# In the last shared-expert group GpSimd splits two weight chunks ahead of the first token gather, and the turns' place in SyncE's load loop moves by two indices

## The chip, the cores and the metric

The kernel runs on one core of a Trainium2 chip. The metric is device time of one execution in microseconds (us). Before the change three runs gave 1834.8, 1836.18 and 1836.39 us, median 1836.18.

The core has five engines, each with an instruction stream of its own, held together by semaphores alone: TensorE (PE; its weight loads are shown as PEld), VectorE (DVE), ScalarE (ACT), GpSimd (POOL) and SyncE (SP), which here only issues DMAs. POOL issues DMAs too: those with indices, and those that add to what is in memory. SPq and POOLq stand for the issuing side of these two engines. An engine works strictly in order: an instruction that waits holds up all that stand behind it.

## The reference, cut to what matters

A decoder layer over x (8 batches, 512 tokens each, width 512), float32:

```
x = x + attn(layernorm(x), queries, combiners)
x = x + cross_attention(layernorm(x), ctx, Wq, bq, Wk, bk, Wv, bv)
x = x + ffn(layernorm(x))
ffn(y):  t = y as 4096 tokens
         probs = softmax(t @ router_w + router_b);  the 2 best of 16 experts per token, weights normed to sum 1
         each expert takes its first 640 tokens: out_e = (silu(h @ w_gate) * (h @ w_up)) @ w_down
         result = y + shared expert(y) + the weighted outputs of the two experts of each token
```

The hidden width is 704. Reaching the precision of float32 takes three matmul passes: each operand is split into a high and a low part, and high*high, high*low and low*high are summed.

## The kernel before, in words

Phase 1 is the attention part. Phase 2 is the feed-forward part. It is a list of 24 groups (`groups`, line 1080). Groups 0 to 7 run the shared expert (job 0) over the 8 batches of 512 tokens. Groups 8 to 23 run the 16 experts (jobs 1 to 16) over 640 gathered tokens each. Every group has six gate/up steps c = 0..5 (matmuls at L72) and then a down projection (L1522) for each tile of 128 tokens. In a step, ACT takes silu of the gate out of PSUM (L1378), DVE multiplies it with up (L1440), ACT writes the high half of the product (`h_hi`, line 1356), and DVE the low half (`h_lo`, line 1417, profile line L1424). The `h_hi` and `h_lo` of step c stand behind silu and product of step c+1. PE's down projection waits for the low half of each step (line 1516).

A job's weights are 17 chunks of 256 KB (`WC`; 11 for gate/up, 6 for down). A chunk n is loaded into one of `RAW` = 6 raw buffers by SP (`load_weights`, line 1234, profile line L1240), its high half is written by ACT (`split`, line 1338, profile line L1336) and its low half by POOL (`split`, line 1276, profile line L1278) into one of `RING` = 22 ring slots. SP's load of chunk n waits until POOL has split chunk n-6 (line 1236). `split_after` (line 1166) gives what is split after which step of which group. In group 7, the last of job 0, chunks 22 and 23 are split after step 0, 24 and 25 after step 1, 26 and 27 after step 2, 28 and 29 after step 3, 30 and 31 after step 4, 32 after step 5, and 33 to 38 after the down projection. ACT does a step's splits one step later: those of step 3 stand behind the `h_hi` of step 3 and in front of silu of step 5 (lines 1386 to 1388). Chunks 22 to 27 have been loaded since SP's turn at group 5 (lines 1258 to 1260). Group 8 needs chunks 17 to 27 for gate/up and 28 to 33 for down.

The tokens of the first expert come so: DVE writes the slot of each token, POOL scatters (token, weight) pairs into a table `slots` (L469), SP reads the table back as `slot_list` (line 1263), POOL gathers the rows of five tiles of 128 tokens by five indirect DMAs (`gather`, line 1284, L1291), SP turns them by five transposing DMAs (`turn_tokens`, line 1216, L1222), and ACT and DVE rebuild float32 halves of them between the down tiles (L1408, L1414, and ACT under L1336). The gather of group 8 (`gather(B)`) stands ahead of all of group 7's splits on POOL. The later gathers stand at the start of the group before.

SP's last loop (lines 1265 to 1270) runs over n = 22, 23, ...; at index i of a job it calls `turn_tokens`, and from n = RING + RAW on it calls `load_weights(n)`.

Of the kernel before, what the change touches and what calls it, by code (L numbers as in the profile page):

```python
# [40 lines left out]
B, S, D = 8, 512, 512  # L41
NT = S // P
# [3 lines left out]
E, K, F = 16, 2, 704  # L46
# [987 lines left out]
def phase2(nc, ctx, a, Y, shared, at, attn):  # L1034
# [7 lines left out]
    TURN_AT = RAW + 4  # L1042

    def sem(name):
        return ctx.enter_context(nc.semaphore(name))
# [29 lines left out]
    s_list = sem("t_list")  # L1075
# [90 lines left out]
    def split_after(g, step):  # L1166


        job, _, _, last = groups[g]
        if g == 0 and step == 3:  # L1170
            return list(range(FIRST, WC))
        if (g, step) in RING_REST:
            return [WC + RING_REST.index((g, step))]
        if not last:
            return []
        done = range(GU, WC) if step == "down" else range(2 * step, min(2 * step + 2, GU))
        return [job * WC + i + RING for i in done if job * WC + i + RING < n_chunks]
# [10 lines left out]
    def adds_of(g, t):  # L1188

        return sum(tiles > t for tiles in tiles_of[:g])  # L1190
# [22 lines left out]
    def sync(sp):  # L1213
        step = attn["sync"](sp)

        def turn_tokens(g):
            sp.wait_ge(s_xg, 16 * gathered[g + 1])
            if gathered[g]:
                sp.wait_ge(s_xtop, gathered[g])
                sp.wait_ge(s_xlow, gathered[g])  # L1220
            for t in range(ET):
                sp.dma_start_transpose(xp[t][:], xn[:, t, :]).then_inc(s_xp, 16)  # L1222

        def load_tokens(g):
            if g == 1:
                filled(sp, "SC", B - 1, NT - 1)
                filled(sp, "V", B - 1, NT - 1)
            else:
                sp.wait_ge(attn["s_ttop"], NT * g)
                sp.wait_ge(attn["s_tlow"], NT * g)  # L1230
                sp.wait_ge(s_gu, unit_no[(g - 2, FC - 1, 0)] + 1)
            step("TURN", g)

        def load_weights(n):
            if n >= RAW:
                sp.wait_ge(s_wl, n - RAW + 1)
            elif n == 0:
                filled(sp, "M", B - 1)
            job, i = divmod(n, WC)
            sp.dma_start(wraw[n % RAW][:], a["wts"][job, :, i * D:(i + 1) * D]).then_inc(s_raw[n % RAW], 16)  # L1240

        for name, b in order:
            if name == "RAW":
                for n in range(RAW):
                    load_weights(n)
            elif name == "WEIGHTS":
                for n in range(*b):
                    load_weights(n + RAW)
            elif (name, b) == ("TURN", 1):
                load_tokens(1)  # L1250
            else:
                step(name, b)
        for stored in attn["s_yout"]:
            sp.wait_ge(stored, 16 * NT * B // 2)
        sp.wait_ge(attn["s_out"], 16 * B)
        for g in range(2, B):
            load_tokens(g)
            if g == 5:
                for n in range(RING, RING + RAW):
                    load_weights(n)  # L1260

        sp.wait_ge(attn["s_scat"], 16 * K * NT * B)
        sp.dma_start(slot_list[:].rearrange("p (e t) k -> p e (t k)", e=E),
                     slots.rearrange("(e p t) k -> p e (t k)", e=E, t=ET)).then_inc(s_list, 16)
        for n in range(RING, n_chunks):
            job, i = divmod(n - RING, WC)
            if i == (0 if job == 0 else TURN_AT) and job < E:
                turn_tokens(B + job)
            if n >= RING + RAW:
                load_weights(n)  # L1270
        sp.wait_ge(attn["s_out"], 16 * B)

    def gpsimd(pool):
        step = attn["gpsimd"](pool)

        def split(n):
            pool.wait_ge(s_wh, n + 1)
            pool.tensor_tensor(wl[n % RING][:], wraw[n % RAW][:], wh[n % RING][:].bitcast(F32),  # L1278
                               ALU.subtract).then_inc(s_wl, 1)

        def rows_at(e, t):
            return bass.IndirectOffsetOnAxis(ap=slot_list[:, e * ET + t, 0:1].bitcast(U32), axis=0)

        def gather(g):

            if g == B:
                pool.wait_ge(s_gu, unit_no[(B - 2, FC - 1, 0)] + 1)
            else:
                pool.wait_ge(s_xp, 16 * gathered[g])
            for t in range(ET):  # L1290
                pool.indirect_dma_start(xn[:, t, :], None, Y[:, :], rows_at(groups[g][1], t),  # L1291
                                        bounds_check=N + PAD - 1).then_inc(s_xg, 16)

        for name, b in order:
            if name == "WEIGHTS":
                for n in range(*b):
                    split(n)
            elif name not in ("RAW",):
                step(name, b)
        for g, (job, part, tiles, last) in enumerate(groups):  # L1300
            if g >= B and g + 1 < NG:
                gather(g + 1)
            if g == B - 1:
                for stored in attn["s_yout"]:
                    pool.wait_ge(stored, 16 * NT * B // 2)
                pool.wait_ge(s_list, 16)
                gather(B)
            for c in range(FC):
                for n in split_after(g, c):
                    split(n)  # L1310
                if (g, c) in scatter_after:
                    step("SCATTER", scatter_after[g, c])
            for t in range(tiles):
                pool.wait_ge(s_ost, tiles_before[g] + t + 1)
                if job == 0:

                    pool.wait_ge(attn["s_out"], 16 * (part + 1))
                    pool.dma_start(out[part * S + t * P:part * S + (t + 1) * P, :], ost[:, t, :],
                                   accum_op=ALU.add).then_inc(s_add[t], 16)
                    continue  # L1320
                if t == 0:

                    for i in range(ET):
                        pool.wait_ge(s_add[i], 16 * adds_of(g, i))
                pool.indirect_dma_start(out[:, :], rows_at(part, t), ost[:, t, :], None,  # L1325
                                        bounds_check=N + PAD - 1, compute_op=ALU.add).then_inc(s_add[t], 16)
            for n in split_after(g, "down"):
                split(n)
        for i in range(ET):
            pool.wait_ge(s_add[i], 16 * adds_of(NG, i))  # L1330
# [194 lines left out]

    block = ctx.enter_context(nc.Block())
    block.sync(sync)
    block.gpsimd(gpsimd)
    block.scalar(scalar)
    block.vector(vector)  # L1530
# [46 lines left out]
```

## Time and profile before

| | |
|---|---|
| three runs, us | 1834.8, 1836.18, 1836.39 (median 1836.18) |
| profiled execution, us | 1836.62 |
| its span from first to last instruction, us | 1834.9 |
| PE busy | 1819.7 us, 99% |
| PEld busy | 1613.0 us, 88% |
| DVE busy | 843.8 us, 46% |
| ACT busy | 754.5 us, 41% |
| POOL busy | 887.1 us, 48% |
| mean granted clock of TensorE | 0.998 |

Group 7 runs on PE from 848.8 to 896.1 us. The timeline view lists merged runs of like instructions: start, length, engine, line, operation, output<-input, count, and in brackets the idle time before it with what ended it. The chain of waits is followed back from the last instruction: start, length, what.

### The profile page before, as it was taken

To read this page: it belongs to the slowest core of one execution; us is meant where nothing else is said; L and a number is where in the kernel's file an instruction comes from. 1 tells how busy PE (TensorE), PEld (TensorE's weight loads), DVE (VectorE), ACT (ScalarE), POOL (GpSimd) and SP (SyncE) were. 2 spreads that over 40 slices of the span, in tenths; PEclk is the share of its full clock that TensorE was granted. 3 is DMA by queue.
4 is the path that set the end of the run, shared out by engine and by line. 5 is a ranking of instruction groups with operands and counts; after the bars stand their busy time and mean duration, and the time that the engine had idled before them with its cause. 6 is when DMAs were issued, how large, how long until landed. Compare 5 with 4: busy or idle time off the path is not lost.

```text
span 1834.9 us, 27134 instructions
## 1 busy us (share of the span) xinstructions
PE 1819.7 (99%) x10104; PEld 1613.0 (88%) x10104; DVE 843.8 (46%) x2028; ACT 754.5 (41%) x1490; POOL 887.1 (48%) x760
## 2 busy tenths in 40 slices
PE   9999999999999999999999999999999999999997
PEld 6888888888887887888899999999999999999996
DVE  6667656765765344343344233442344323443242
ACT  4544434444554333332444434443344434444331
POOL 2443444335553232224655666555665656556631
PEclk9999999999999999999999999999999999999999
DMA  8431342233452233223766666676666676666722
GB/s 311 167 105 65 126 144 98 81 110 110 115 138 40 37 41 81 47 46 60 184 125 153 155 148 140 127 164 152 141 143 131 163 153 134 144 139 164 144 41 29
DMA packets 216274, 219.90 MB, mean 120 GB/s; under 512 B 133680, under 2 KB 133680, under 8 KB 214864
## 3 DMA queue, kind: packets, MB, share of 16 engines
q1 hardware_dynamic: 190848, 165.07, 32.8%
q0 software_dynamic: 25296, 53.11, 16.9%
q8 instruction: 80, 1.31, 0.3%
q14 instruction: 50, 0.41, 0.1%
HBM read 138.80 MB, written 49.97 MB: 103 GB/s over the span
## 4 chain that ended last, share of the span: by engine, by line
PE 93%; issue 4%; DMA 1%; SPq 1%; DVE 0%; POOL 0%; ACT 0%; POOLq 0%; DVEq 0%; ACTq 0%
PE ps L72 64%; PE ps L1522 22%; PE ps L866 4%; PE ps L872 1%; PE ps L1007 1%; PE ps L891 1%; DMA slot_list<-slots 0%; SPq L1222 0%; SPq L353 0%; DMA buffer<-in_wts 0%; DMA buffer<-tokens_normed,slot_list 0%; PE ps L967 0%; POOL buffer L1291 0%; DMA buffer<-in_WkT 0%; PE ps L943 0%
## 5 line engine op out<-in xcount | busy, mean ns | idle before, releaser
L72 PE MATMUL ps<-buffer,buffer 128*128 128x320 f32 (+1 forms) x6900 | 1240.5, 341 | 1.2 <-DVE buffer L719 0.8
L72 PEld LDWEIGHTS ps<-buffer,buffer 128*128 128x128 f32 x6900 | 1120.6, 188 | 106.8 <-issue 1.5
L1278 POOL TENSOR_TENSOR buffer<-buffer,buffer 128x512 fp32r<-128x512 f32 x289 | 379.4, 1478 | 250.1 <-ACT buffer L1336 249.8
L1522 PE MATMUL ps<-buffer,buffer 128*128 128x512 f32 x1904 | 437.8, 390 | 1.4 <-DVE buffer L1424 1.4
L1522 PEld LDWEIGHTS ps<-buffer,buffer 128*128 128x128 f32 x1904 | 355.7, 188 | 76.1 <-POOL buffer L1278 2.2
L1336 ACT ACTIVATE buffer<-buffer 128x512 fp32r<-128x512 f32 (+1 forms) x491 | 294.3, 652 | 166.2 <-PE ps L1522 93.7
L1378 ACT ACTIVATE buffer<-ps 128x320 f32<-128x320 f32 (+1 forms) x240 | 112.7, 469 | 598.6 <-PE ps L72 571.0
L1440 DVE TENSOR_TENSOR ps<-ps,buffer 128x320 f32<-128x320 f32 (+2 forms) x198 | 100.2, 506 | 490.5 <-ACT buffer L1378 462.7
L1325 POOL DMA_INDIRECT out_tokens<-buffer,slot_list x80 | 125.8, 1573 | 185.6 <-DVE buffer L1470 137.3
L469 POOL DMA_INDIRECT slots<-pairs,slot_u x64 | 63.6, 994 | 182.0 <-DVE slot_u L853 164.9
L477 ACT ACTIVATE buffer<-ps 128x512 fp32r<-128x512 f32 (+1 forms) x148 | 81.9, 603 | 107.6 <-PE ps L72 59.8
L482 ACT ACTIVATE buffer<-buffer,shift,rstd 128x512 f32<-128x512 f32 x96 | 70.6, 808 | 102.8 <-DVE shift L647 102.8
L1470 DVE TENSOR_SCALAR buffer<-ps,slot_list 128x512 f32<-128x512 f32 x80 | 59.7, 746 | 112.2 <-PE ps L1522 112.2
L1424 DVE TENSOR_TENSOR buffer<-ps,buffer 128x320 fp32r<-128x320 f32 (+2 forms) x198 | 96.8, 489 | 10.2 <-ACT buffer L1336 9.2
L442 POOL TENSOR_TENSOR buffer<-buffer,buffer 128x512 f32<-128x512 f32 x32 | 42.1, 1351 | 116.2 <-DVE shift L647 105.4
L1291 POOL DMA_INDIRECT buffer<-tokens_normed,slot_list x80 | 83.6, 1046 | 29.7 <-issue 29.7
L1336 ACT ACTIVATE buffer<-ps 128x320 fp32r<-128x320 f32 (+2 forms) x198 | 86.5, 437 | 0.3 <-DVE ps L1440 0.3
L1440 DVE TENSOR_TENSOR buffer<-ps,buffer 128x512 f32<-128x512 f32 (+1 forms) x42 | 29.0, 690 | 97.7 <-ACT buffer L1378 93.5
L1408 DVE COPY buffer<-buffer 128x512 uint16<-128x512 uint16 x80 | 73.1, 936 | 0.5
L431 POOL TENSOR_TENSOR buffer<-buffer,buffer 128x512 fp32r<-128x512 f32 x28 | 35.2, 1298 | 71.8 <-ACT buffer L477 71.8
L629 DVE BATCH_NORM_STATS2 stats<-buffer 128x6 f32<-128x512 f32 x96 | 61.3, 685 | 7.9 <-DMA buffer<-in_x 7.3
L477 ACT ACTIVATE buffer<-buffer 128x512 fp32r<-128x512 f32 (+1 forms) x104 | 59.8, 679 | 3.9 <-DMA buffer<-in_ctxT 2.2
(126 smaller groups left out, 1058.1 us busy)
## 6 DMA issues: line engine op xcount, KB each, us to landing
buffer<-in_wts SPq DMA_DIRECT2D x289, 256.0 KB
buffer<-in_xT SPq DMA_DIRECT2D x8, 1024.0 KB, 5.5
buffer<-in_ctxT SPq DMA_DIRECT2D x8, 1024.0 KB, 7.8
out_tokens<-buffer SPq DMA_DIRECT2D x8, 1024.0 KB, 4.4
tokens_normed<-buffer SPq DMA_DIRECT2D x32, 256.0 KB, 2.8
out_tokens<-buffer POOLq DMA_DIRECT2D x32, 256.0 KB, 5.6
buffer<-in_x SPq DMA_DIRECT2D x7, 1024.0 KB, 5.4
buffer<-combiners_top SPq DMA_DIRECT2D x6, 1024.0 KB, 7.6
```

The lines of the kernel that those rows point to most:

```text
L72: last = pe.matmul(out, left, right, start=(c == 0 and i == 0), stop=(c == len(parts) - 1 and i == 2))
L477: return act.activation(dst, src, ACT.Copy)
L866: last = pe.matmul(out, left, right, start=(i == 0), stop=(i == len(pairs) - 1))
L1278: pool.tensor_tensor(wl[n % RING][:], wraw[n % RAW][:], wh[n % RING][:].bitcast(F32), ALU.subtract).then_inc(s_wl, 1)
L1291: pool.indirect_dma_start(xn[:, t, :], None, Y[:, :], rows_at(groups[g][1], t), bounds_check=N + PAD - 1).then_inc(s_xg, 16)
L1325: pool.indirect_dma_start(out[:, :], rows_at(part, t), ost[:, t, :], None, bounds_check=N + PAD - 1, compute_op=ALU.add).then_inc(s_add[t] ...
L1336: return act.activation(dst, src, ACT.Copy)
L1378: act.activation(silu[u % TMP][0:rows_of(c), 0:n], bank[0:rows_of(c), 0:n], ACT.Silu)\
L1408: dve.tensor_copy(halves_of(t)[:, :, :, 0], xp[t][:, NC:2 * NC, :]).then_inc(s_xlow, 1)
L1424: dve.tensor_tensor(lo[:, first:first + n], product_of(u)[0:rows, 0:n], hh[0:rows, c, first:first + n].bitcast(F32), ALU.subtract).then_in ...
L1440: dve.tensor_tensor(product_of(u)[0:rows_of(c), 0:n], up_bank[u % 2][rows, 0:n], silu[u % TMP][0:rows_of(c), 0:n], ALU.mult).then_inc(s_ht, 1)
L1522: ins = pe.matmul(down_bank[n % 2][:], left, right, start=(c == 0 and i == 0), stop=(c == FC - 1 and i == len(passes) - 1))
```

## The change

On POOL the block that waits for the stored tokens and for `slot_list` and then issues `gather(B)` moves from the head of group 7 to behind the splits that belong to step 0 of group 7, which are those of chunks 22 and 23. On SP the index at which `turn_tokens(B)` is called in the last loop changes from 0 to 2.

```
@@ sync
         for n in range(RING, n_chunks):
             job, i = divmod(n - RING, WC)
-            if i == (0 if job == 0 else TURN_AT) and job < E:
+            if i == (2 if job == 0 else TURN_AT) and job < E:
                 turn_tokens(B + job)
             if n >= RING + RAW:
                 load_weights(n)
@@ gpsimd
             if g >= B and g + 1 < NG:
                 gather(g + 1)
-            if g == B - 1:
-                for stored in attn["s_yout"]:
-                    pool.wait_ge(stored, 16 * NT * B // 2)
-                pool.wait_ge(s_list, 16)
-                gather(B)
             for c in range(FC):
                 for n in split_after(g, c):
                     split(n)
+                if (g, c) == (B - 1, 0):
+                    for stored in attn["s_yout"]:
+                        pool.wait_ge(stored, 16 * NT * B // 2)
+                    pool.wait_ge(s_list, 16)
+                    gather(B)
                 if (g, c) in scatter_after:
                     step("SCATTER", scatter_after[g, c])
```

## Rows read from the trace of the kernel before

**Rows 1.** The page, busy time by engine and the chain's shares.
```profile
PE 1819.7 (99%) x10104; PEld 1613.0 (88%) x10104; DVE 843.8 (46%) x2028; ACT 754.5 (41%) x1490; POOL 887.1 (48%) x760
PE 93%; issue 4%; DMA 1%; SPq 1%; DVE 0%; POOL 0%; ACT 0%; POOLq 0%; DVEq 0%; ACTq 0%
```
**Rows 2.** Timeline of PE, end of group 7; in brackets idle time before.
```profile
878.71 2.88 PE L1522 MATMUL ps<-buffer,buffer 128*128 128x512 f32 x12
882.70 0.93 PE L1522 MATMUL ps<-buffer,buffer 128*128 128x512 f32 x3 [1.10 <-DVE buffer L1424]
883.97 12.28 PE L1522 MATMUL ps<-buffer,buffer 128*128 128x512 f32 x53 [0.34 <-DVE buffer L1424]
```
**Rows 3.** Chain of waits in order of time (start, us, what), 845 to 882.
```profile
849.55 9.13 DMA slot_list<-slots
...
865.16 3.80 DMA buffer<-tokens_normed,slot_list
...
877.35 4.62 DMA buffer<-in_wts
```
**Rows 4.** Timeline of SP's queue, 845 to 880.
```profile
868.97 6.76 SPq L1222 DMA_TRANSPOSE buffer<-buffer  x5
875.78 3.17 SPq L1240 DMA_DIRECT2D buffer<-in_wts  x6
```
**Rows 5.** Timeline of ACT in group 7.
```profile
860.90 1.16 ACT L1336 ACTIVATE buffer<-buffer 128x512 fp32r<-128x512 f32 x2
...
871.79 1.15 ACT L1336 ACTIVATE buffer<-buffer 128x512 fp32r<-128x512 f32 x2
...
879.13 0.64 ACT L1336 ACTIVATE buffer<-buffer 128x512 fp32r<-128x512 f32 x1 [1.78 <-DMA buffer<-in_wts]
...
880.45 0.58 ACT L1378 ACTIVATE buffer<-ps 64x512 f32<-64x512 f32 x1
```
**Rows 6.** Timeline of POOL, 848 to 882.
```profile
859.70 1.15 POOL L1291 DMA_INDIRECT buffer<-tokens_normed,slot_list  x1 [7.65 <-issue]
...
865.16 1.01 POOL L1291 DMA_INDIRECT buffer<-tokens_normed,slot_list  x1 [0.30 <-issue]
866.20 5.04 POOL L1278 TENSOR_TENSOR buffer<-buffer,buffer 128x512 fp32r<-128x512 f32 x4
872.50 2.54 POOL L1278 TENSOR_TENSOR buffer<-buffer,buffer 128x512 fp32r<-128x512 f32 x2 [1.26 <-ACT buffer L1336]
```
**Rows 7.** Timeline of POOL at the next gather, that of group 9.
```profile
897.84 7.85 POOL L1278 TENSOR_TENSOR buffer<-buffer,buffer 128x512 fp32r<-128x512 f32 x6
905.87 1.12 POOL L1291 DMA_INDIRECT buffer<-tokens_normed,slot_list  x1 [0.17 <-issue]
```
**Rows 8.** Line L1222 (the turns), issue to landing; timelines of DVE and PE.
```profile
DMA to landing us min/median/max: 3.1/3.3/3.4
...
883.86 2.77 DVE L1408 COPY buffer<-buffer 128x512 uint16<-128x512 uint16 x2
893.04 0.69 DVE L1414 TENSOR_TENSOR buffer<-buffer,buffer 128x512 fp32r<-128x512 f32 x1
...
896.09 38.88 PE L72 MATMUL ps<-buffer,buffer 128*128 128x320 f32 x264
```
**Rows 9.** Timeline of PE at its end; windows there (stretch, us, busy, PEclk, DMA).
```profile
1819.66 4.69 PE L1522 MATMUL ps<-buffer,buffer 128*128 128x512 f32 x20
...
1826.00:1827.00 1.00, 0.00 (x0) 0.00 (x0) 0.00 (x0) 0.00 (x0) 1.00 (x1) 1.00 0.19 31
1827.00:1828.00 1.00, 0.00 (x0) 0.00 (x0) 0.00 (x0) 0.00 (x0) 0.48 (x1) 0.61 0.00 0
1828.00:1834.00 6.00, 0.00 (x0) 0.00 (x0) 0.00 (x0) 0.00 (x0) 0.00 (x0) 0.50 0.34 44
```
**Rows 10.** Timeline of PE at the kernel's start.
```profile
1.08 3.17 PE L878 MATMUL ps<-ones 128*128 128x128 bf16 x28 [1.08 <-POOL ones L377]
4.49 11.49 PE L891 MATMUL ps<-buffer,buffer 128*128 128x512 f32 x26 [0.24 <-DMA buffer<-in_WkT]
```

More of the change, by code:

```diff
@@ L1266, in sync @@
             job, i = divmod(n - RING, WC)
-            if i == (0 if job == 0 else TURN_AT) and job < E:
+            if i == (2 if job == 0 else TURN_AT) and job < E:
                 turn_tokens(B + job)
@@ L1302, in gpsimd @@
                 gather(g + 1)
[L1303 to L1307, printed above, removed]
             for c in range(FC):
@@ L1310, in gpsimd @@
                     split(n)
+                if (g, c) == (B - 1, 0):
+                    for stored in attn["s_yout"]:
+                        pool.wait_ge(stored, 16 * NT * B // 2)
+                    pool.wait_ge(s_list, 16)
+                    gather(B)
                 if (g, c) in scatter_after:
```

## The prediction

> **What bounds the kernel now.** I read the page first: PE is busy 99% of the span, and the chain that ended last is 93% PE [rows 1]. So every us by which PE idles longer comes on top, and nothing that POOL, ACT or SP save elsewhere counts unless PE idles there. Then I asked the timeline of PE for the stretch that the change touches. Group 7's gate/up ends where the first 12 down matmuls begin at 878.71. These end near 881.6, PE idles 1.10 us, does 3 matmuls, idles 0.34 us, and then runs through [rows 2]. Both gaps end with DVE's low half of the product. These 1.44 us are PE's only idle time in the group.
>
> The chain of waits says what is behind the gap, and here it leaves PE for 35 us: the read of the slot list (9.13 us from 849.55, landed at 858.68), the gathers, the last of which lands 3.80 us after it started at 865.16, SP's turns, SP's weight loads, one of which lands at 881.97, and behind it ACT and DVE, at whose work PE's gap ends [rows 2, 3]. SP's queue shows the join: five turns from 868.97, the weight loads right behind at 875.78 [rows 4]. The first of them is chunk 28. ACT's timeline shows its use: ACT idles 1.78 us for a landing in_wts chunk and starts its split at 879.13; silu of step 5 comes behind it at 880.45 [rows 5], and the high and low halves of step 4, which PE waits for, come behind that silu. So PE does not need chunk 28 until the down projection of group 8, but ACT, working in order, passes on its lateness at once. The end of this chain has no slack: it is already late by 1.44 us of PE time.
>
> **SP's edit.** The loop starts at n = 22, and load_weights is called from n = 28 on. The iterations 22 and 23 (indices 0 and 1) therefore issue nothing, and neither do 24 to 27. Turns at index 2 stand in the same place of SP's queue as turns at index 0: behind the read of the list, ahead of the load of chunk 28. Cost and gain are 0 from both sides, for the instruction streams are equal. No load goes ahead of the turns.
>
> **POOL's edit, before.** The list is there at 858.68 [rows 3]. The first gather starts at 859.70, the fifth at 865.16 for 1.01 us, so the gathers end at 866.17. Splits 22 to 25 follow in one run of four [rows 6]. The turns start at 868.97, which is 2.80 us after the last gather's end [rows 4, 6].
>
> **POOL's edit, after.** The gather now stands behind splits 22 and 23, which wait for ACT's halves of these chunks. ACT writes them from 860.90, and that is set by PE's pace (behind silu of step 1), not by POOL [rows 5]. Where ACT starts a pair at 871.79, POOL starts its own at 872.50, 0.71 us later [rows 5, 6]. So POOL's split 22 starts at 860.90 + 0.71 = 861.61. Two splits take 2.54 us [rows 6], which gives 864.15. From a split to a following gather whose waits are met it takes 0.18 us (897.84 + 7.85 = 905.69 to 905.87) [rows 7]. The first gather starts at 864.33 and not at 859.70: a shift of 4.63 us. The upper bound is the form seen before, 1.02 us from release to gather, which gives 5.5. The lower bound comes if POOL's splits started with ACT's: 3.9. I take 4.6, for the two rows used are the same instructions with the same neighbours.
>
> **What hangs on the gather.** The five gathers, their landing, the five turns and the loads behind are the same work in the same order, so all move by 4.6: turns from 873.6, load of chunk 28 at 875.78 + 4.63 = 880.4, ACT's split 28 at 883.8 (before 879.13), silu of step 5 at 885.1, and PE's gap ends at 887.3 and not at 882.70. PE still reaches the gap at 881.6, since its first 12 down matmuls need only steps 0 to 3, which are done. The gap is 1.10 + 4.63 = 5.7 us, and the 0.34 behind it stays. Nothing gives it back: before, PE has no more idle time from here on in which it could be saved [rows 2].
>
> What is hidden. Splits 24 to 27 on POOL move behind the gathers: gathers from 864.33 for the same 6.47 us end at 870.8, splits 24 and 25 at 873.3, 26 and 27 at 875.9. Loads up to chunk 33 wait for split 27, and SP comes to them after 880.4, so 4.5 us of cover remain. The turned tokens land at most 3.4 us after issue; before, the last was issued some 5.4 us after 868.97, landing at 877.8; after, at 882.4. DVE's use at 883.86 moves to 888.5. The last low half of them is done at 893.73, PE wants it at 896.09 [rows 8]; both move together and keep 2.4 us. If that cover were gone, PE would wait the difference at the head of group 8, but both hang on the same late `h_lo`.
>
> **The clock.** A gap of 5.7 us on PE is five times the one that is there now [rows 2]. What a long one does can be seen at the end alone: PE's last matmul ends at 1824.35, the granted clock is 1.00 until 1827, has a mean of 0.61 in the next us, which puts the fall near 1827.2, and is 0.50 (1.2 GHz) from then on [rows 9]. PE had been idle for 2.9 us there, and here it would be for 5.7. The price of coming back is seen at the start: 28 matmuls of 128 columns take 3.17 us, 113 ns each, while 53 of 512 columns take 12.28 us, 58 ns per 128 columns [rows 10, 2]. By these durations the stretch ran at half pace (1.2 GHz). Of a stretch of 3.17 us at half pace, half is lost: 1.6 us. Bounds: 0 (the clock holds) and twice that, 3.2 us. I take 1.6, the one stretch that the trace has.
>
> The Trainium skill (TensorE: Matmul & The Clock Gate, "What's actually happening") says of this: "the default state is throttled, and activity releases the throttle". The trace agrees at both ends. Its table of what to do asks for matmuls without long gaps in mid-kernel; no stretch of this trace shows a fall and a recovery in mid-kernel, so by that rule the sum has the clock term, and without it the sum is 4.6.
>
> **Sum.** 4.6 + 1.6 = 6.2 us. On the profiled execution's own time 1836.62 (span 1834.9 and 1.7 around it) that is 1842.8. The median of the runs is 0.44 lower: 1836.18 + 6.2 = 1842.4, or +0.34%. The forecast is slower.
>
> **Rivals.**
>
> A. The late turns without the clock. The gap is there, but the clock holds at 2.4 GHz. For it: the granted clock stays at 1.00 for 2.9 us of idling at the end [rows 9], and where the fall comes may differ between executions. Against it: 5.7 is twice 2.9. Time: 1836.18 + 4.6 = 1840.8.
>
> B. The loads do go in front of the turns, by two. If chunks 28 and 29 were raw before ACT comes to them, ACT would next wait for chunk 30, issued first behind the turns at 880.4 and landing as chunk 28 did 3.35 us after issue [rows 4, 5], at 883.8, with chunk 31 some 0.7 us later; split 31 and the high half of step 5 would end near 885.7, the low half at 886.4. PE would idle 4.1 us before the step-5 matmuls where it now idles 1.44: +2.7, 1838.9. Against it is the plain reading of the loop: n >= 28.
>
> C. Not slower: the wait for the list covers the two splits. POOL idles 7.65 us ahead of the first gather [rows 6]. If the list lands later than POOL's split 23 ends (864.15), the splits fill idle time and the gather starts when it did. It decides from a list that lands 5.5 us later than in the profile. Then the time is 1836.2; and if, besides, an earlier split 24 or an earlier raw buffer took away ACT's wait, at most the whole 1.44 us of PE's gaps could go: 1834.7. Against it: the list landed at 858.68, and the runs' spread of 1.6 us leaves no room for a list 5.5 us later, as that would have lengthened the kernel before by the same chain.
>
> D. The clock costs twice as much: half pace for twice the start's stretch, 1836.18 + 4.6 + 3.2 = 1844.0. For it: the waits around the gap leave PE with 3 matmuls and a further short gap before steady work.
>
> **How the numbers follow.** The forecast 0.49, A 0.26, D 0.08, B 0.06, C 0.11. The forecast's own spread is 1841.3 to 1843.5. The range from 1838.2 to 1844.5 holds the forecast, A, D and B, 0.89 by their chances, and some 0.8 with the uncertainty of their sizes. A measurement of this kernel can tell about 0.2% from no change, that is 3.7 us, so slower means above 1839.85. The forecast, D and most of A lie there: 0.49 + 0.08 + 0.20 = 0.77. Same: the rest of A, B and most of C: 0.06 + 0.06 + 0.08 = 0.20. Faster: 0.03.
>
> **What would show it.** In the changed profile: POOL's timeline has two L1278 from about 861.6, then the first L1291 near 864.3; SP's turns start near 873.6 and the loads follow at once near 880.4, with none between 849.6 and 873; ACT waits some 6.4 us for in_wts and starts at 883.8; PE's gap ahead of the second run of L1522 is 5.7 us; a window over 884 to 892 shows a granted clock under 1 and matmuls near 460 ns. Wrong: a weight load ahead of the turns (B), a list landing past 864 (C), or a gap with clock 1.00 (A). What would upset all is a first gather under 860, or a gap that stays near 1.1 us in spite of late turns.

## The result and the profile after

The changed kernel takes 1843.03 us in the median of 7 runs (1840.93 to 1845.03), against 1835.21 (1834.39 to 1836.39) before. The ratio is 1.0042, 95% interval [1.0032, 1.0052]: slower, by 7.8 us in the medians. The prediction was 1842.4, +6.2, range 1838.2 to 1844.5. The profiled execution took 1843.07 us, span 1841.4.

Timeline of GpSimd in the changed kernel, then of SyncE's queue and of ACT.

```profile
861.59 2.53 POOL L1278 TENSOR_TENSOR buffer<-buffer,buffer 128x512 fp32r<-128x512 f32 x2 [9.56 <-ACT buffer L1336]
864.29 1.14 POOL L1291 DMA_INDIRECT buffer<-tokens_normed,slot_list  x1 [0.17 <-issue]
...
869.77 1.02 POOL L1291 DMA_INDIRECT buffer<-tokens_normed,slot_list  x1 [0.30 <-issue]
870.82 5.04 POOL L1278 TENSOR_TENSOR buffer<-buffer,buffer 128x512 fp32r<-128x512 f32 x4
```

```profile
849.52 0.38 SPq L1263 DMA_DIRECT2D slot_list<-slots  x1
873.63 6.76 SPq L1222 DMA_TRANSPOSE buffer<-buffer  x5
880.45 9.52 SPq L1240 DMA_DIRECT2D buffer<-in_wts  x10
```

```profile
860.88 1.15 ACT L1336 ACTIVATE buffer<-buffer 128x512 fp32r<-128x512 f32 x2
...
883.93 0.63 ACT L1336 ACTIVATE buffer<-buffer 128x512 fp32r<-128x512 f32 x1 [6.62 <-DMA buffer<-in_wts]
884.80 0.63 ACT L1336 ACTIVATE buffer<-buffer 128x512 fp32r<-128x512 f32 x1 [0.24 <-DMA buffer<-in_wts]
885.34 0.57 ACT L1378 ACTIVATE buffer<-ps 64x512 f32<-64x512 f32 x1
```

Against [rows 6], the first gather moved from 859.70 to 864.29. It is preceded by two splits of 1.27 us, and before them GpSimd idles 9.56 us for ACT, whose splits came when they did before (860.88 against 860.90 [rows 5]). Against [rows 4], turns and loads moved from 868.97 and 875.78 to 873.63 and 880.45. No load stands between the slot list and the turns: SyncE's half of the change moved nothing. ACT's wait for chunk 28 grew from 1.78 to 6.62 us. A second wait of 0.24 us, for chunk 29, is new, and silu of step 5 moved by 4.89.

Timeline of PE in the changed kernel, and its granted clock (columns of the windows, here and below: stretch, us, busy and count of PE, PEld, DVE, ACT, POOL, then granted clock, DMA share, GB/s).

```profile
878.69 2.88 PE L1522 MATMUL ps<-buffer,buffer 128*128 128x512 f32 x12
887.58 15.20 PE L1522 MATMUL ps<-buffer,buffer 128*128 128x512 f32 x56 [6.01 <-DVE buffer L1424]
902.62 2.65 PE L72 MATMUL ps<-buffer,buffer 128*128 128x320 f32 x17
```

```profile
884.00:886.00 2.00, 0.00 (x0) 0.00 (x0) 0.00 (x0) 1.76 (x4) 1.36 (x2) 0.87 0.95 347
886.00:888.00 2.00, 0.42 (x1) 0.45 (x2) 1.45 (x3) 2.00 (x5) 2.00 (x2) 0.50 0.87 288
888.00:890.00 2.00, 2.00 (x6) 1.44 (x6) 1.97 (x3) 1.73 (x3) 2.00 (x3) 0.50 0.63 166
890.00:892.00 2.00, 2.00 (x7) 1.52 (x6) 2.00 (x3) 1.85 (x4) 1.05 (x1) 0.50 0.70 231
892.00:894.00 2.00, 2.00 (x9) 1.63 (x8) 1.47 (x3) 1.77 (x4) 1.01 (x1) 0.92 0.48 145
894.00:896.00 2.00, 2.00 (x10) 1.68 (x9) 0.89 (x2) 0.30 (x1) 0.00 (x0) 1.00 0.86 108
```

The gap in the second line answers to the 1.10 us of [rows 2]: it is 6.01 us. The gap of 0.34 in front of step 5's matmuls is gone. Step 5's low half starts 1.20 us after step 4's (DVE at 886.74 and 887.94), and PE, at half clock, takes some 1.4 us over step 4's three matmuls (8 of them take 3.75 us), so it no longer waits. The granted clock falls to 0.50 (1.2 GHz) while PE idles and is back at 1.00 soon after 892. In the stretches of 2 us PE gets 6 and 7 matmuls done and not the 10 of the last line.

One measure serves all runs below: the **down stretch** of group 7, from its first down matmul to the first matmul of group 8. Before: 878.71 to 896.09 = 17.38 us [rows 2, 8]. After: 878.69 to 902.62 = 23.93 us, that is +6.55, of which the gaps account for 6.01 - 1.44 = 4.57 and the slower matmuls for the other 2.0. Counted by place, the first gap adds 4.91, and all behind it (step 4's three matmuls, step 5's gap, the rest up to group 8) 1.65. The spans differ by 6.5, so nothing else of note moved.

### The profile page after: what moved, and what is told of

Read it like the earlier page. It is cut to its first block, busy times and chain, and to the rows that moved or that the text cites. A ratio compares the mean times of both kernels' runs of the same rounds, so it can differ in the third digit from the quotient of the medians.

```text
span 1841.4 us, 27134 instructions
## 1 busy us (share of the span) xinstructions
PE 1822.0 (99%) x10104; PEld 1614.9 (88%) x10104; DVE 843.3 (46%) x2028; ACT 752.9 (41%) x1490; POOL 887.6 (48%) x760
## 4 chain that ended last, share of the span: by engine, by line
PE 96%; DMA 1%; DVE 1%; SPq 1%; issue 1%; POOL 0%; ACT 0%; POOLq 0%; ACTq 0%; DVEq 0%
PE ps L72 66%; PE ps L1522 24%; PE ps L866 4%; PE ps L872 1%; PE ps L1007 1%; DMA buffer<-means 0%; SPq L1222 0%; DMA buffer<-in_x 0%; DMA means<-mean 0%; DMA buffer<-tokens_normed,slot_list 0%; DMA buffer<-in_wts 0%; POOL buffer L1291 0%; DVE buffer L280 0%; PE ps L943 0%; DVE buffer L719 0%
```

## The experiments

All eleven ran with a profile and in five rounds against the kernel before. The medians of before beside them were 1835.2 (sp_only, pool_only, keep_busy, late_splits_after), 1835.21 (the two doses and the two loads_ahead) and 1835.47 (the two loads4 and splits_between). The ratio compares the two kernels over the rounds. In the table, gap is PE's idle time within the down stretch.

| kernel | first gather | gap, us | clock in the stretch | down stretch, us | median, us | ratio [95%] |
|---|---|---|---|---|---|---|
| before (its profile) | 859.70 | 1.10 + 0.34 | 1.00 | 17.38 | 1835.21 | |
| sp_only | 857.38 | 0.15 | 1.00 | 15.85 | 1835.31 | 0.9998 [0.9989, 1.0006] |
| changed kernel | 864.29 | 6.01 | falls | 23.93 | 1843.03 | 1.0042 [1.0032, 1.0052] |
| pool_only | 863.62 | 5.78 + 0.38 | falls | 23.92 | 1842.34 | 1.0034 [1.0021, 1.0047] |
| keep_busy | 863.98 | 0.87 + 0.43 | 1.00 | 22.19 | 1840.76 | 1.0027 [1.0017, 1.0037] |
| dose_one | 862.55 | 4.12 | falls | 21.69 | 1840.82 | 1.0033 [1.0022, 1.0043] |
| dose_four | 869.37 | 11.04 | falls | 29.40 | 1848.10 | 1.0068 [1.0054, 1.0082] |
| loads_ahead_after | 863.49 | 3.62 | falls | 20.95 | 1840.93 | 1.0030 [1.0019, 1.0041] |
| late_splits_after | 864.18 | none; 5.80 in group 8 | 1.00 here, falls in group 8 | 15.44 | 1842.22 | 1.0033 [1.0021, 1.0044] |
| loads4_after | 864.53 | 0.15 + 0.65 | 1.00 | 16.80 | 1836.09 | 1.0001 [0.9992, 1.0010] |
| splits_between | 862.81 | none | 1.00 | 15.42 | 1834.22 | 0.9994 [0.9985, 1.0003] |
| loads_ahead_before | 856.84 | 0.16 | 1.00 | 15.83 | 1834.87 | 0.9997 [0.9988, 1.0006] |
| loads4_before | 858.91 | 0.16 | 1.00 | 15.82 | 1834.67 | 0.9996 [0.9987, 1.0005] |

### The two halves of the change

pool_only is the changed kernel with SyncE's index back at 0; sp_only is the kernel before with index 2.

```
-            if i == (0 if job == 0 else TURN_AT) and job < E:      # sp_only has this edit alone;
+            if i == (2 if job == 0 else TURN_AT) and job < E:      # pool_only has all but this one
```

> Only GpSimd's half of the change; SyncE's turns stay at index 0. Theory (the whole cost comes from the gather behind two splits): the same as the changed kernel, about 1842 to 1844 us, against about 1835.2 before; first gather at 864.3, turns at 873.6, one gap of 6.0 us on PE. Rival (SyncE's edit has a part in it): clearly nearer to 1835.

> Only SyncE's half of the change; the gather stays in front. Theory: the loop issues nothing for its first six indices, so the instruction streams are those of the kernel before: ratio 1.000 within 0.1%, which also gives the noise of a comparison. Rival (two loads do go out in front of the turns, as in rival B): the turns start some 0.9 us later and ACT's wait of 1.78 us for the first chunk goes, up to 1.4 us faster.

pool_only has the full cost, 1.0034, its interval overlapping that of the change, and sp_only has none, 0.9998. The rival for each falls. The second gap of pool_only (0.38 us, at half clock) has its own cause: ACT waits 0.59 us more for a weight chunk in front of the high half of step 5. But sp_only's profile holds what the prediction had not seen. Its instruction streams are those of the kernel before, and its trace differs. Timelines of POOL and PE of sp_only:

```profile
857.38 1.14 POOL L1291 DMA_INDIRECT buffer<-tokens_normed,slot_list  x1 [5.43 <-issue]
```

```profile
878.61 3.56 PE L1522 MATMUL ps<-buffer,buffer 128*128 128x512 f32 x15
882.33 12.29 PE L1522 MATMUL ps<-buffer,buffer 128*128 128x512 f32 x53 [0.15 <-DVE buffer L1424]
894.46 30.81 PE L72 MATMUL ps<-buffer,buffer 128*128 128x320 f32 x209
```

The gather starts 2.3 us earlier than in the profile of before, and PE's gaps are 0.15 us and not 1.44. The cause is the read of the slot list, whose line in the two traces (before, then sp_only) says:

```profile
DMA to landing us min/median/max: 9.1/9.1/9.1
DMA to landing us min/median/max: 6.9/6.9/6.9
```

In sp_only the gather starts 1.02 us behind that landing, as before, and ACT waits for no weight chunk any more. Over the 13 traces of this case the same small transfer took 6.1 to 7.1 us in nine, and 8.5, 8.5, 9.1 and 9.2 in four. The profile of before was one with a late list. The execution that gave sp_only's trace took 1835.20 us, like the median of before; that of before took 1836.62. Against sp_only the change adds 23.93 - 15.85 = 8.1 us to the down stretch, and the medians say 7.8.

### Is the clock a term of the sum?

```
+                    if (g, t, c) == (B - 1, 0, FC - 2):
+                        pe.wait_ge(s_ht, unit_no[(g, FC - 2, 0)] + 1)
+                        for _ in range(KEEP):          # KEEP = 22
+                            pe.matmul(gate_bank[unit_no[(g, FC - 2, 0)] % 2][:], hh[:, 0, cols],
+                                      wh[(base + GU) % RING][:], start=True, stop=True)
                     if t == 0:
                         pe.wait_ge(s_wl, m + 1)
```

> The changed kernel, with 22 more matmuls (of 128x512, results into a bank that is free then, used by nothing) on PE between the down matmuls of steps 3 and 4 of the first tile of group 7, where the gap is. 22 x 0.23 = 5.1 us, less than the gap. Theory (6.0 us of late work plus some 2 us of half clock behind the gap): the granted clock stays at 1.00, PE's idle time falls to about 0.9 + 0.3 us, the 0.34 us gap in front of step 5 comes back, and the time falls by 2 to 3 us to about 1840 (1835.2 + 4.6). Rival (the clock in the record costs nothing, the rest is something else): stays at 1843.

Timeline of PE in keep_busy, and its clock over the same time:

```profile
878.36 2.88 PE L1528 MATMUL ps<-buffer,buffer 128*128 128x512 f32 x12
881.08 5.15 PE L1518 MATMUL ps<-buffer,buffer 128*128 128x512 f32 x22
887.10 0.94 PE L1528 MATMUL ps<-buffer,buffer 128*128 128x512 f32 x3 [0.87 <-DVE buffer L1425]
888.46 12.25 PE L1528 MATMUL ps<-buffer,buffer 128*128 128x512 f32 x53 [0.43 <-DVE buffer L1425]
```

```profile
884.00:888.00 4.00, 3.13 (x13) 1.99 (x11) 1.76 (x3) 3.92 (x8) 3.63 (x3) 1.00 0.85 296
888.00:892.00 4.00, 3.57 (x17) 2.98 (x17) 3.97 (x5) 3.50 (x7) 2.83 (x3) 1.00 0.72 198
```

The work of step 4 resumes as late as in the changed kernel (887.10 against 887.58), the clock holds, the small gap comes back, and the down stretch is 1.7 us shorter than in the changed kernel. The medians differ by 2.3 us from the changed kernel, by 1.6 from pool_only, which ran beside it. From the resumed work to group 8 keep_busy takes 13.45 us and the changed kernel 15.04, which is 1.6. So the clock's term is 1.6 to 2.3 us, shown by an edit that fills the gap and leaves the late chain as it is.

### Does the cost follow the gather's start?

dose_one puts one split ahead of the gather, dose_four four.

```
# dose_one
-                for n in split_after(g, c):
+                for k, n in enumerate(split_after(g, c)):
+                    if (g, c, k) == (B - 1, 0, 1):
+                        (the gather's four lines, as in the change)
                     split(n)
-                if (g, c) == (B - 1, 0):
-                    (the same four lines)
# dose_four
-                if (g, c) == (B - 1, 0):
+                if (g, c) == (B - 1, 1):
```

> As the changed kernel, but only chunk 22 is split ahead of the first gather; 23 comes behind it. Theory: gather at 863.0, all behind it 3.4 us later than before, PE's gap 1.44 + 3.4 = 4.8 us; the clock still falls, for the gap is longer than the 2.9 us of idling after which it fell at the end of the kernel, and costs some 2 us: about 1840.5. Rival (the clock only falls after a gap nearer to 6 us): 1838.6.

> As the changed kernel, but four chunks (22 to 25) are split ahead of the first gather, which then stands behind step 1's splits. Theory: ACT's split 24 starts at 866.3, GpSimd's at 867.0, both done at 869.6, gather at 869.75, that is 10.05 us later than before and 5.45 later than in the changed kernel; PE's gap 11.5 us; the cost of the clock does not grow with the gap, so the time is 1843.0 + 5.45 = 1848.5. Rival (part of the cost is one that does not follow the gather's start): off that line by over 1.5 us.

Timelines of PE, dose_one and then dose_four:

```profile
885.19 14.85 PE L1522 MATMUL ps<-buffer,buffer 128*128 128x512 f32 x56 [4.12 <-DVE buffer L1424]
```

```profile
892.26 15.64 PE L1522 MATMUL ps<-buffer,buffer 128*128 128x512 f32 x56 [11.04 <-DVE buffer L1424]
```

dose_one came out at 1840.82 (expected 1840.5), dose_four at 1848.10 (1848.5). The gap goes 4.12, 6.01, 11.04 with one, two and four splits, while what is lost behind it stays small: 56 matmuls and the way to group 8 take 14.69, 15.04 and 15.48 us (885.19 to 899.88, 887.58 to 902.62, 892.26 to 907.74). So the late start is paid one for one, and the clock about once. Both gaps came out shorter than expected (4.12 for 4.8, 11.04 for 11.5 us). The clock fell in dose_one too, as expected: 0.87 over 884 to 886 and 0.50 over 886 to 888.

### What the change's words say, done

```
             if i == (2 if job == 0 else TURN_AT) and job < E:
+                if job == 0:
+                    for m in range(RING + RAW, RING + RAW + 2):    # loads4_after and loads4_before: + 4
+                        load_weights(m)
                 turn_tokens(B + job)
-            if n >= RING + RAW:
+            if n >= RING + RAW + 2:
                 load_weights(n)
```

> The changed kernel, and SyncE does what the change's words say: it issues the loads of chunks 28 and 29 ahead of the turns. Theory (rival B of the prediction, worked out there): ACT's splits 28 and 29 wait for nothing, the turns start at 873.7, ACT next waits for chunk 30, PE has one gap of some 4 us in front of step 5's matmuls; +2.7 us by the gap, plus up to 2 us of clock if it falls: 1838 to 1840. Rival (any load behind the turns holds ACT as long): 1843.

> The changed kernel (gather behind splits 22 and 23), with the loads of chunks 28 to 31 issued ahead of the turns; the last of them waits for split 25, which ends near 873.3, when the turns would start anyway. Theory (the cost of the late gather is only the lateness of the loads that ACT meets in front of silu of step 5 and the high half of step 5): ACT waits for none of the four; it waits up to 2 us for chunk 32, behind the high half of step 5, where the 2 to 4 us of slack of group 8's tokens cover it; PE's gap is under 0.4 us, clock 1.00, time 1835 to 1836, as before. Rival (the late gather itself, by the tokens, costs time): 1837 or more.

Timeline of PE in loads_ahead_after, and its clock; then PE in loads4_after:

```profile
877.89 3.56 PE L1525 MATMUL ps<-buffer,buffer 128*128 128x512 f32 x15
885.07 13.93 PE L1525 MATMUL ps<-buffer,buffer 128*128 128x512 f32 x53 [3.62 <-DVE buffer L1427]
```

```profile
884.00:886.00 2.00, 0.93 (x4) 0.83 (x5) 1.73 (x3) 1.72 (x4) 2.00 (x3) 1.00 0.98 330
886.00:888.00 2.00, 2.00 (x8) 1.59 (x7) 2.00 (x3) 2.00 (x5) 0.94 (x1) 0.64 0.69 228
888.00:890.00 2.00, 2.00 (x6) 1.52 (x6) 1.36 (x3) 1.85 (x4) 1.01 (x1) 0.51 0.47 137
```

```profile
878.93 3.56 PE L1525 MATMUL ps<-buffer,buffer 128*128 128x512 f32 x15
882.65 4.57 PE L1525 MATMUL ps<-buffer,buffer 128*128 128x512 f32 x19 [0.15 <-DVE buffer L1427]
887.87 8.02 PE L1525 MATMUL ps<-buffer,buffer 128*128 128x512 f32 x34 [0.65 <-DVE buffer L1468]
895.73 9.54 PE L72 MATMUL ps<-buffer,buffer 128*128 128x320 f32 x64
```

Two loads ahead do what rival B said: 15 and not 12 down matmuls run through, then one gap of 3.62 us in front of step 5's (4.1 predicted). The clock falls after this gap too, and the median of 1840.93 lies just above the expected 1838 to 1840. That profiled execution was the fastest of its seven (1839.12), so what its clock cost may not be what it costs in the median.

With four loads ahead no cost can be measured any more, 1836.09 and 1.0001 [0.9992, 1.0010], with the gather as late (864.53) as in the changed kernel. ACT's one wait is 2.30 us for chunk 32, behind the high half of step 5. It shows at PE as 0.65 us between the down tiles: DVE waits 2.48 us for ACT's token half, and its copy L1468, which frees PE's bank, stands behind. The gaps of 0.80 us in all are more than the 0.4 expected, and the down stretch is 0.95 us longer than sp_only's.

### Are late loads harmful by ACT's order alone?

```
         done = range(GU, WC) if step == "down" else range(2 * step, min(2 * step + 2, GU))
+        if g == B - 1 and step in (3, 4, 5):
+            return []
+        if g == B - 1 and step == "down":
+            done = range(6, WC)                                   # chunks 28 to 38
```

> The changed kernel, with the splits of chunks 28 to 32 taken out of group 7's steps 3 to 5 and put at the head of its splits after the down projection, on ACT and GpSimd. The gather, the turns and the loads stay as late as in the changed kernel. Theory (late loads cost only because ACT, in order, waits for chunk 28 in front of silu of step 5): PE's gap goes altogether, clock 1.00, turned tokens land near 882.4, in time; the time is 1835.2 + 0 - 1.4 = about 1834, at most 1835.5. Rival (the late turns themselves hold up the tokens of group 8): the gap moves to the head of group 8 or between the down tiles, 1838 or more.

This expectation failed: 1842.22 is where the rival's number lay (1838 or more). The gap did leave the down stretch, which at 15.44 us is as short as any. It came back in the next group. PE's timeline and the chain of waits of late_splits_after:

```profile
894.02 7.20 PE L72 MATMUL ps<-buffer,buffer 128*128 128x320 f32 x48
907.01 18.28 PE L72 MATMUL ps<-buffer,buffer 128*128 128x320 f32 x110 [5.80 <-DVE ps L1444]
```

```profile
895.21 0.85 POOL out_tokens L1322
896.05 6.30 POOL buffer L1282 x5
902.35 0.02 issue
902.37 3.01 DMA buffer<-in_wts
905.38 0.02 issue
905.40 0.02 ACT buffer L1340
```

I had moved GpSimd's splits behind the output stores as well. The loads of chunk 34 and on wait for GpSimd's split six chunks back, so they were late in their turn, and ACT met them in front of silu of group 8, in order as ever. The chain runs through weights (in_wts) and not through the late tokens, so the rival has the place right and the cause wrong. Both variants of the stall are ACT waiting for a chunk that nobody needs for tens of us. What was wrong is my edit, and the next one mends it: ACT splits one chunk behind each token step, GpSimd splits them in front of the stores.

```
+        if g == B - 1 and step in (3, 4, 5):
+            return [28, 29, 30, 31, 32] if step == 5 else []      # GpSimd: in front of the output stores
...
             for m in split_after(g, FC - 1):                      # ACT
-                split(m)
+                if g != B - 1:
+                    split(m)
...
                     x_hi(gx, t)
+                    if g == B - 1:
+                        split(28 + t)                             # ACT: one behind each token step
```

> The changed kernel, loads as late as there, but chunks 28 to 32 are split by ACT one each behind the five token steps of group 7's tail, and by GpSimd in front of the output stores. It mends what went wrong in the trial that put these splits behind the whole tail, where the six raw buffers came free too late. Theory (order on ACT): no gap in front of step 4's down matmuls; five splits of 0.63 us lengthen the token chain, which may cost PE up to 2 us at the head of group 8 or between down tiles: 1835.2 to 1837.5. Rival (late loads cost wherever the splits stand): 1840 or more.

Timeline of PE in splits_between:

```profile
877.21 15.59 PE L1527 MATMUL ps<-buffer,buffer 128*128 128x512 f32 x68
892.63 12.62 PE L72 MATMUL ps<-buffer,buffer 128*128 128x320 f32 x85
```

All 68 down matmuls run without a gap, group 8 follows at once, and the median is 1834.22, ratio 0.9994 [0.9985, 1.0003], below the band I gave (1835.2 to 1837.5), as the five extra splits lengthened nothing that PE waits for. Loads and turns are as late here as in the changed kernel (turns 5.1 us ahead of PE's first down matmul in both: 872.07 and 877.21, 873.63 and 878.69). So the lateness by itself costs nothing: the 8 us come from the place of the splits. The edit moves those of both engines; that ACT's are the ones that count is read from the changed kernel's trace (its wait of 6.62 us in front of silu), and no run moved ACT's alone.

### Candidates

> The kernel before (gather in front), and SyncE issues the loads of chunks 28 and 29 ahead of the turns. They go out at about 867.5 and 868.7, behind GpSimd's splits 22 and 23, and the turns at about 869.2, 0.2 us later than before; chunk 30 is issued near 876.1 and lands near 879.5. Theory: ACT waits for nothing or some 0.2 us, PE's gaps of 1.44 us go: about 1833.9. Rival (no gain, a later wait takes its place): 1835.2.

> The kernel before (gather in front), with the loads of chunks 28 to 31 ahead of the turns. A candidate for the best version: it takes away ACT's wait also when the slot list lands late (9.1 us after issue, as in the profile of the kernel before, not 6.1 to 7.1). Where the list lands early there is only 0.2 us to gain: 1834.8 to 1835.2, no difference that can be measured.

Both intervals hold 1: 0.9997 and 0.9996. loads4_before (1834.67) lies near the expected 1834.8 to 1835.2. The 1833.9 expected of loads_ahead_before were missed, and 1834.87 is nearer to the rival's 1835.2: the expectation counted on taking away 1.44 us of gaps, and with a list that lands early, as in its trace (6.6 us), the kernel before hardly has them. With splits_between there are three versions whose medians lie 0.3 to 1.3 us under that of before and none that can be told from it. The profile of loads4_before is of use all the same: its list landed late (8.5 us), its gather started at 858.91, and PE's gap was 0.16 us, where the kernel before had 1.44 with 859.70. That is one trace, and its gather was 0.8 us earlier.

## Why the prediction came out as it did

- **SyncE's edit issues nothing.** Right: same place of the turns in the trace, sp_only 0.9998.
- **The gather starts at 864.33.** Right: 864.29, and with it turns (873.6 predicted, 873.63), loads (880.4, 880.45), ACT's split (883.8, 883.93) and silu (885.1, 885.34). The price of two splits and 0.18 us was read off rows of the same instructions in the same neighbourhood.
- **The gap is 5.7 us and nothing gives it back.** Right in kind, 6.01 measured. The missing 0.3 is mostly ACT's new wait of 0.24 us for chunk 29: I had moved silu by the same 4.6 as the loads, and it moved by 4.89.
- **Clock: it falls, 1.6 us.** Right in kind, and the size is near: the slower matmuls cost 2.0 us, of which 0.34 replace the old gap in front of step 5, and keep_busy gives 1.6 to 2.3. Luck has a part in it. The 1.6 was half of a stretch of 3.17 us at the kernel's start, taken by its durations alone (the record shows a granted clock of 1.00 there), while here some 4.7 us with PE at work ran at 0.50, from 887.58 to about 892.3. By the rule of the Trainium skill (TensorE: Matmul & The Clock Gate, "What's actually happening") idling throttles and activity releases; the trace agrees now in mid-kernel too. Rival A, where the clock holds, is refuted for the profiled executions. Its 1840.8 is about what keep_busy shows. Rival D, a clock that costs 3.2 us, lies outside keep_busy's 1.6 to 2.3.
- **The sum on the median.** This is the mis-sized term. I carried 4.6 us over as the difference to a kernel that idles 1.44 us at this place. That was true of the profiled execution (+6.5 in the span, 6.2 predicted) but that one had its slot list 2 us later than most. Where the list lands in 6 to 7 us, the kernel before has a gap of about 0.15, as sp_only's trace shows, and the change costs 8.1. So +6.2 stands against +7.8 in the medians. The changed kernel does not gain from an early list, since its gather waits for ACT. The sign of it stood in the data that I had: the profiled run was the slowest of before at 1836.62, above all three runs. That the time forecast is so near (1842.4, measured 1843.03) is luck in part: the median of three that I started from, 1836.18, is 0.97 above that of seven, and this makes up for most of the 1.6 us by which the difference was too small.
- **Rival C** asked for a list 5.5 us later than 858.68. In 13 traces it took at most 9.2 us from issue, as late as in the profile. I argued against it from the runs' spread of 1.6 us. That was weak: three runs are few, and in later rounds single runs of before took up to 1841.2 us. No trace of such a run was kept, so what made it long is open. Against C stand the traces.
- **Rival B** could not be in this kernel, but its mechanism and size held when built (3.62 us of gap against 4.1).

## What to carry to other kernels

Work that an in-order engine does early for a later group is a trap when its input can be late: ACT split chunk 28 more than 50 us before PE wanted it (group 8's down projection starts at 941.34) and held up, in doing so, what PE wanted at 881.6, some 4 us after ACT had begun to wait. Put such work behind the urgent instruction, or issue its load ahead of anything that waits for something else; and when moving it, follow the ring buffers that it frees, or the stall turns up one group on. And when a wait in the profile ends with a small DMA, take its duration from several executions before a prediction counts from it.

## What the runs showed that I had not expected

The read of an 80 KB list by one DMA landed 6.1 to 9.2 us after issue, at the same place of SyncE's stream in all 13 traces; why is open. In loads_ahead_after PE idled 3.62 us to 885.07 and the granted clock was still 1.00 over 884 to 886; it fell (0.64, then 0.51) only when PE was at work again. So a gap can be paid for after it has ended. The seven runs of the changed kernel spread over 4.1 us, the seven of before beside them over 2.0, but in later rounds 20 to 27 runs of before spread over 4.0 to 6.8 us. What makes these spreads is open.
